# Attention in a fused layer: four single PSUM banks for the products of the row maximum, three for the scores, and one exponential per head

## The reference

```
hn = layernorm(x, ln1_g, ln1_b)
q, k, v = (hn @ wq + bq), (hn @ wk + bk), (hn @ wv + bv)     # split in 16 heads of 16
scores = einsum('bhqd,bhkd->bhqk', q, k) / sqrt(16)
attn = softmax(scores, axis=-1)
o = einsum('bhqk,bhkd->bhqd', attn, v)
...
x = x + o @ wo + bo         # then layernorm, argmax over 8 experts, the chosen expert's FFN
```

## Time and profile before

| | before |
|---|---|
| median of 3 runs | 3639.58 us (3636.05 to 3642.61) |
| the profiled execution, own time | 3635.68 us |
| its span | 3634.0 us |
| granted TensorE clock, mean | 0.894 |
| first and last value product of attention | 1498.6 and 2924.1 us |
| PE, DVE, ACT busy over the span | 83%, 72%, 48% |

### The profile page before, as it was taken

One profiled execution on the slowest core, in us unless ns is written; L12 is line 12 of the kernel. 1 busy time (PEld: TensorE's weight loads), 2 busy tenths in 40 slices (PEclk: granted clock), 3 DMA queues, 4 the chain that ended last, 5 costly groups with the idle time before them and its releaser, 6 DMA issues. The chain is left out here.

```text
span 3634.0 us, 43270 instructions
## 1 busy us (share of the span) xinstructions
PE 3014.5 (83%) x12860; PEld 1434.6 (39%) x12860; DVE 2601.1 (72%) x3622; ACT 1729.3 (48%) x2113; POOL 816.1 (22%) x397
## 2 busy tenths in 40 slices
PE   5668788787797775999999999999999957669994
PEld 3333234343343332433333333333333324658883
DVE  5526989789889896998989898989899638111111
ACT  2225554554544541376767676767677720101110
POOL 2204455455455465000000000000000015210003
PEclk9888899898898887799999999999999965589997
DMA  4532112111121124744545454445454044044554
GB/s 151 164 115 88 65 65 81 63 66 66 57 75 68 54 75 53 132 67 63 68 57 69 59 69 61 66 62 67 59 66 54 7 123 117 21 157 156 170 173 127
DMA packets 230405, 306.67 MB, mean 84 GB/s; under 512 B 111467, under 2 KB 179332, under 8 KB 215748
## 3 DMA queue, kind: packets, MB, share of 16 engines
q1 hardware_dynamic: 225988, 291.60, 35.3%
q0 software_dynamic: 4224, 12.59, 1.2%
HBM read 240.38 MB, written 63.21 MB: 84 GB/s over the span
## 5 line engine op out<-in xcount | busy, mean ns | idle before, releaser
L701 DVE TENSOR_REDUCE attn_mx<-attn_pX 128x1 f32<-128x512 f32 x2048 | 1271.0, 683 | 156.7 <-PE attn_pX L609 154.8
L681 ACT ACTIVATE attn_pr<-attn_pS 128x1024 f32<-128x1024 f32 x1024 | 992.8, 1022 | 500.0 <-PE attn_pS L622 499.4
L609 PE MATMUL attn_pX<-attn_ks,attn_qs 48*128 48x512 f32 x2048 | 749.8, 491 | 75.4 <-DMA attn_vs<-v_d 25.2
L1150 PE MATMUL mamba_pY<-mamba_g,mamba_ident 128*128 128x512 f32 x1024 | 523.4, 660 | 213.9 <-DVE mamba_g L1274 213.8
L1261 DVE TENSOR_TENSOR_SCAN mamba_h<-mamba_pA,mamba_hs,mamba_db 128x512 f32<-128x512 f32 x512 | 617.2, 1264 | 95.3 <-ACT mamba_pA L1004 90.3
L609 PEld LDWEIGHTS attn_pX<-attn_ks,attn_qs 48*128 48x128 f32 x2048 | 304.4, 190 | 773.2 <-DVE attn_mx L701 708.9
L945 POOL TENSOR_TENSOR mamba_db<-mamba_bq,mamba_u 128x2048 f32<-128x2048 f32 x128 | 577.8, 4515 | 72.5 <-DVE mamba_u L1221 72.2
L1004 ACT ACTIVATE mamba_pA<-mamba_dt,mamba_an 128x512 f32<-128x512 f32 x512 | 352.0, 691 | 456.2 <-DVE mamba_h L1261 455.9
L632 PE MATMUL attn_pO<-attn_pr,attn_vs 128*17 128x512 f32 x4096 | 549.5, 609 | 0.4 <-ACT attn_pr L681 0.4
L622 PE MATMUL attn_pS<-attn_qs,attn_ks 50*128 50x512 f32 x2048 | 467.7, 413 | 34.0 <-issue 19.8
L1150 PEld LDWEIGHTS mamba_pY<-mamba_g,mamba_ident 128*128 128x128 f32 x1024 | 209.4, 211 | 513.9 <-DVE mamba_g L1274 274.7
(11 more groups left out here) (170 smaller groups left out, 2027.5 us busy)
## 6 DMA issues: line engine op xcount, KB each, us to landing
mamba_bq<-bc_d SPq DMA_DIRECT2D x64, 1024.0 KB, 4.7
attn_ks<-parts_d SPq DMA_DIRECT2D x192, 256.0 KB, 9.3
exp_w<-in_w SPq DMA_DIRECT2D x46, 1024.0 KB, 4.9
attn_vs<-v_d SPq DMA_DIRECT2D x32, 544.0 KB, 15.5
parts_d<-proj_qp SPq DMA_DIRECT2D x32, 512.0 KB, 3.0
attn_qs<-parts_d SPq DMA_DIRECT2D x192, 64.0 KB, 8.3
attn_qs<-attn_mt SPq DMA_DIRECT2D x512, 1.0 KB
oraw_d<-attn_oe SPq DMA_DIRECT2D x32, 256.0 KB, 2.1
```

The costliest lines, as they stand in the source:

```text
L609: pe.matmul(pX[bank(s, n)][:, :], QS[slot][rows, pair, qt * P:(qt + 1) * P], KS[slot][rows, pair, part * BANK:(part + 1) * BANK], start=Tr ...
L681: act.activation(PR[2 * (kt % 2) + pair][:, :, :], pS[pair][:, :, :], ACT.Exp, scale=HD ** -0.5).then_inc(p_sb, 1)
L701: dve.tensor_reduce(MX[:, col:col + 1], pX[bank(s, n)][:, :], AX.X, ALU.max).then_inc(x_max, 1)
L1150: mm = pe.matmul(pY[j][:, :], ident[:, :], G[k % 2][:, n, :], start=False, stop=(q == NQ - 1 and n == QN - 1))
```

## The change

`pX` has 4 banks in place of 3. `pS` is 3 single banks in place of 2 double ones. Each head has its own exponential of 512 columns, and its own wait. The score products of a step go to the 3 banks in turn, so a score product waits for the exponential three places before it (`score_freed`). The counter of finished exponentials becomes two, for even and odd places. TensorE's order within a step changes: one head's score product, one X product, in turn; and the score product of the fourth head now stands behind the value products.

```diff
--- before.py
+++ after.py
@@ -449,9 +449,11 @@
     NG = batches * HEADS // GH
     NI = NG * QC
     RING = 4
-    NX = 3
+    NX = 4
+    NS = 3
     NSM = GH * QT * QC
     SM_KT = NSM // KT
+    NSC = GH * KT
     PAIRS = GH // 2
     MROWS = 2
     STACK_M = STACK + MROWS
@@ -472,7 +474,7 @@
         MS = m.sb("ms", [P, MROWS, GH * QT], F32R)
         MT = [m.sb(f"mt{n}", [P, 32]) for n in range(2)]
         ZERO = m.sb("zero", [P, slots_d.shape[1]])
-        pS = [m.ps(f"pS{n}", [P, 2, BANK]) for n in range(2)]
+        pS = [m.ps(f"pS{n}", [P, BANK]) for n in range(NS)]
         pX = [m.ps(f"pX{n}", [P, BANK]) for n in range(NX)]
         pO = m.ps("pO", [P, BANK])
         ops_in = [m.sem(f"ops_in{s}") for s in range(RING)]
@@ -486,7 +488,7 @@
         m_split = m.sem("m_split")
         m_turned = m.sem("m_turned")
         s_ps = m.sem("s_ps")
-        p_sb = m.sem("p_sb")
+        p_sb = [m.sem(f"p_sb{n}") for n in range(2)]
         pv_done = m.sem("pv_done")
         o_sb = m.sem("o_sb")
         o_out = [m.sem(f"o_out{n}") for n in range(2)]
@@ -501,6 +503,16 @@
                 return n - NX + 1
             before = [k - NSM for k in range(NSM) if bank(s - 1, k) == bank(s, n)]
             return max(before) + 1
+
+        def score_bank(s, n):
+
+            return (s % RING + n) % NS
+
+        def score_freed(s, n):
+
+            if n >= NS:
+                return n - NS
+            return max(k - NSC for k in range(NSC) if score_bank(s - 1, k) == score_bank(s, n))
 
         def order(n):
 
@@ -610,22 +622,23 @@
                                   KS[slot][rows, pair, part * BANK:(part + 1) * BANK],
                                   start=True, stop=True).then_inc(x_ps, 1)
 
-                def scores(i, s, kt, pair):
+                def scores(i, s, kt, h):
 
                     _, _, slot, use = where(i, s)
-                    if kt == 0 and pair == 0:
+                    if kt == 0 and h == 0:
                         pe.wait_ge(mrow_in[slot], use * MROW_IN + 2 * MROW_IN)
-                    z = s * 2 * KT + kt * 2 + pair
-                    pe.wait_ge(p_sb, i * (RING * 2 * KT) + (z + 1))
-                    for h in range(2):
-                        rows = slice(h * HALF, h * HALF + STACK_M)
-                        mm = pe.matmul(pS[pair][:, h, :], KS[slot][rows, pair, kt * P:(kt + 1) * P],
-                                       QS[slot][rows, pair, :], start=True, stop=True)
-                    mm.then_inc(s_ps, 1)
+                    n = kt * GH + h
+                    pair, half = divmod(h, 2)
+                    rows = slice(half * HALF, half * HALF + STACK_M)
+                    last = score_freed(s, n)
+                    pe.wait_ge(p_sb[last % 2], i * (RING * NSC // 2) + (s * NSC // 2 + last // 2 + 3))
+                    pe.matmul(pS[score_bank(s, n)][:, :], KS[slot][rows, pair, kt * P:(kt + 1) * P],
+                              QS[slot][rows, pair, :], start=True, stop=True).then_inc(s_ps, 1)
 
                 def values(i, s, kt):
 
-                    pe.wait_ge(p_sb, i * (RING * 2 * KT) + (s * 2 * KT + kt * 2 + 4))
+                    for n in range(2):
+                        pe.wait_ge(p_sb[n], i * (RING * NSC // 2) + (s * NSC // 2 + kt * 2 + 4))
                     if kt == 0:
                         pe.wait_ge(o_sb, i * RING + (s + 2))
                     for h in range(GH):
@@ -638,8 +651,8 @@
                 scores_max(0, 0, 0, NSM)
                 scores_max(0, 1, 0, LEAD)
                 pe.wait_ge(ones_ready, 2 * RING)
-                scores(0, 0, 0, 0)
-                scores(0, 0, 0, 1)
+                for h in range(GH):
+                    scores(0, 0, 0, h)
 
                 def maxima_ahead(i, s, left, n0, n1):
 
@@ -649,16 +662,20 @@
                     elif left >= 2:
                         scores_max(i, s + 2, n0 + LEAD - NSM, n1 + LEAD - NSM)
 
+                assert SM_KT == GH
+
                 def body(i, s, left):
                     for kt in range(KT):
                         n = kt * SM_KT
                         ahead = [(i, s, kt + 1)] if kt + 1 < KT else [(i, s + 1, 0)] if left >= 1 else []
-                        for pair in range(2):
+                        for h in range(GH - 1):
                             if ahead:
-                                scores(*ahead[0], pair)
-                            maxima_ahead(i, s, left, n + pair * SM_KT // 4, n + (pair + 1) * SM_KT // 4)
+                                scores(*ahead[0], h)
+                            maxima_ahead(i, s, left, n + h, n + h + 1)
                         values(i, s, kt)
-                        maxima_ahead(i, s, left, n + SM_KT // 2, n + SM_KT)
+                        if ahead:
+                            scores(*ahead[0], GH - 1)
+                        maxima_ahead(i, s, left, n + GH - 1, n + GH)
                 bodies(pe, body)
 
             @block.scalar
@@ -670,16 +687,18 @@
                     act.wait_ge(pv_done, i * (RING * KT) + (s * KT + 2))
                     act.copy(OE[n][:, :], pO[:, :]).then_inc(o_sb, 1)
 
-                act.sem_inc(p_sb, 2)
+                for n in range(2):
+                    act.sem_inc(p_sb[n], 2)
                 act.wait_ge(o_sb, 1)
 
                 def body(i, s, left):
                     for kt in range(KT):
                         act.wait_ge(pv_done, i * (RING * KT) + (s * KT + kt + 1))
-                        for pair in range(2):
-                            act.wait_ge(s_ps, i * (RING * 2 * KT) + (s * 2 * KT + kt * 2 + pair + 1))
-                            act.activation(PR[2 * (kt % 2) + pair][:, :, :], pS[pair][:, :, :], ACT.Exp,
-                                           scale=HD ** -0.5).then_inc(p_sb, 1)
+                        for h in range(GH):
+                            n = kt * GH + h
+                            act.wait_ge(s_ps, i * (RING * NSC) + (s * NSC + n + 1))
+                            act.activation(PR[2 * (kt % 2) + h // 2][:, h % 2, :], pS[score_bank(s, n)][:, :],
+                                           ACT.Exp, scale=HD ** -0.5).then_inc(p_sb[n % 2], 1)
                         if kt == 0:
                             copy_out(i, s)
                 bodies(act, body)
```

## The result

The changed kernel takes 3749.58 us, the median of 4 runs (3743.35 to 3793.66), against 3637.82 for the kernel before: 1.0335 times, 95% interval 1.0267 to 1.0404. Slower, as forecast, but by 112 us where I had 60 to 63; 3749.58 lies at the very end of the range that I gave. The profiled execution took 3743.35 us, its span is 3741.7, 107.7 more than before.

The account below looks back on a forecast made before the run. The loop of X products and VectorE reductions bound the kernel (2.69 us per step), to be replaced by a score loop of 2.83. Terms sum to +62.8 us: 3635.7 + 62.8 = 3698.5, predicted as 3700, range 3645 to 3750.

Parts of the forecast that it names:

- The X loop and its opening: X products and VectorE's reductions through three banks set the old step, 2.68 us by terms; a fourth bank opens this loop.
- The score loop, 2.83: Score product, X product, value products, fourth head's score product and last exponential form a closed loop of 2.83 us per step.
- The 468 steps: Attention steps left after taking off the last items', edge and half-clock steps; each grows from 2.69 to 2.83, +65.5 us.
- Halving costs nothing by itself: On ScalarE, the four extra exponential starts per step are hidden in idle time; 0.16 us per step were ScalarE the bound.
- Splits, -20: Steps with a split of maxima, one per item: VectorE's slack and the extra bank absorb the 0.70 us stall, -20 us.
- The last item, +8.9: Last item's steps, without X products, grow from 2.00 to 2.59 us: 15 x 0.59; five steps before it come back.
- Half-clock steps, +5.4: 16 steps behind the phase's start and loop edges lengthen from 4.13 to 4.47 us, +5.4 us.
- rival 4: One more 0.1 us delay per step, from value products' waits or more frequent half clock: +47 us, 3747; chance 0.11.
- Edges, +3: Restart at seven loop edges: an X product between last score product and values costs 0.43 us each, +3 us.
- 1: Rival: banks decouple the engines, so the step falls to VectorE's 2.40 us, about 3510 us in all; chance 0.07.
- rival 2: X product runs beside the score product, free in the score loop: step 2.59 us, 3586 us in all; chance 0.04.
- 3: Rival: the score loop closes at its short end, 2.74 us, 3656 to 3660, or 2.70 and 3640; chance 0.12.

Follow-up runs that it names:

- e4: Changed kernel with a zero bias from SBUF on each exponential, making it longer; fastest run 3783.7 us, the others 3858 to 4064, no ratio given.
- f1: Changed kernel with the X product before the value products moved ahead of the third head's score product; 3631.98 us, ratio 0.9980 to the kernel before.
- e1: Changed kernel with 3 X banks instead of 4; median 3898 us, fastest 3796.5 us, for that run alone ratio 1.0719 to the kernel before.
- e3: Kernel before with each 1024-column exponential split into two of 512, banks and order kept; 3639.75 us, ratio 1.0009.
- e2: Changed kernel with the fourth head's score product ahead of the value products instead of behind them; 3655.98 us, ratio 1.0050 to the kernel before.
- f2: Changed kernel with two of each step's four X products computed twice into the same bank; 3717.5 us, ratio 1.0213 to the kernel before.
- f3: Changed kernel with the hardware loop over the attention's rings written out, so without edges; 3694.5 us, ratio 1.0165 to the kernel before.
- g1: f1 with the ring loop written out and both sets of banks numbered on through all items; 3601.2 us, ratio 0.9885 to the kernel before.
- g3: Changed kernel's own order, ring loop written out, banks numbered on, unread filling products in the last item; 3673.1 us, ratio 1.0101 to the kernel before.
- g2: g1 plus filling X products in the last item, into idle banks that nobody reads; 3580.6 us, ratio 0.9845 to the kernel before.
- f4: Kernel before with the hardware loop over the attention's rings written out; 3602.8 us, ratio 0.9906.

## Why the prediction was right or wrong

**The X loop and its opening.** Right. With the loop of 2.68 open, VectorE does idle more and not less, since the score loop took over.

**The score loop, 2.83.** Right in length and in its terms. The step measures 2.83; ScalarE's gap is 0.77, where I had "about 0.6", and VectorE's 0.34, where I had "about 0.4": small misses in rows that follow from the step. e4 moved the step by the exponential's growth, f1 by the X product's 0.24, e1 showed the other loop next behind it. The term with no row of before, the exponential at 0.60, measured 0.604. The last item's 2.59 and the half-clock step's 4.47 came out too. The 468 steps made +66 us, as summed.

**Halving costs nothing by itself.** Right where ScalarE has slack, shown by e3.

**Splits, -20.** Right: -19.3. A step with a split is 0.09 over the others.

**The last item, +8.9.** Right for the profiled execution, with the five steps ahead of it +8.3 in all. That was partly luck: in the profiles of e2, f1, f2, f3 and g1 it ran at half clock, and the last 22 steps took 80 to 84 us there against 58 in the changed kernel's profile. Whether the slower of the changed kernel's four runs (3754.84 and 3793.66 us, granted clocks 0.877 and 0.865) had that or longer low stretches isn't known, as only one was profiled.

**Half-clock steps, +5.4.** This is the step that failed. I wrote "16 at half clock (two behind the phase's start and each edge)" and put the change into their length alone, 0.34 each. The length was right; the number was wrong, and I took it to be the same on both sides. The kernel before had 11, the changed one 35, and the term is +40. f2 gave the engine more to do in the same steps and their number fell to 10; f3 took away the edges, and outside the phase's start and the last item they vanished. What decides how long one stretch gets stays open: e1, with half-clock steps of 4.56, had five short ones and one of 92.2 us. I had the thought in rival 4, "a half clock that comes more often as TensorE idles more", and priced it as 0.1 us on every step. It is not on every step: it is 1.6 us on each step for which the clock stays down. That rival 4's 3747 lies so near the measured 3749.6 is luck, for its 0.1 on each of 468 steps did not come.

**Edges, +3.** Too small: +9.6. I counted seven stalls where there are six, and one slot of an X product at each. The first score product's wait at a ring's end, 7 x 0.48 = 3.4, and the fourth head's wait behind ScalarE's own stall, seen at 1885.37, came on top: the six stalls with it are 6.2 us longer in all.

Together the half-clock steps (35 us more than forecast) and the edges (6.6 more) are all but 3 us of what the forecast of +62.8 lacks on the +107.7 measured in the span. The table counts the 0.14 of all 511 steps in its first row, the forecast counted it in the terms of those steps; in the forecast's own terms the two misses are 37 and 7.6 us.

**The rivals.** 1, 2 and 3 did not come, as the step is 2.83; the 2.59 of rival 2 is real, but only with the X product elsewhere. A loop through the value products was left even with the fourth head ahead of them (e2), so three score banks did not give VectorE's 2.40 in any of the three orders run.

## What to carry to other kernels

Where engines hand banks round, the step is the longest closed path through a wait, and a product that stands in program order between two waits of that path is paid in full: one X product that took 0.24 us of each step made 92 us here (g3 against g2). Adding a bank opens one loop; before counting the gain, close the next one, from the place of each product in the engine's order. And count the steps at half clock as a result of the change, not as a property of the place: here the clock stayed down long after the stall at which it fell, in some executions and not in others, and more work on the same path went with shorter stretches.

## What the runs showed of the hardware that I had not expected

- The low clock's stretch behind the same stall differs from kernel to kernel and from edge to edge. It was 3.4 to 10.2 us in the kernel before (half-clock steps up to 4.13 us), and up to 13.7 us in e2 and f1 (up to 4.07). With 4.47 us it was 10.2 to 34.1 us (changed), with 4.55 and 4.56 us mostly 3.4 to 10.2 but once 300 us (e4) and once 92 us (e1). With two X products more per step at an unchanged step it was 3.4 to 10.2 us (f2). Behind edges, stretches over 13.7 us came only with half-clock steps of 4.47 us or more and no added products; these are six edges or fewer of one profile each.
- The times spread with the granted clock: 3634 to 3645 us over 13 runs of the kernel before at 0.891 to 0.895; 3743 to 3794 at 0.880 to 0.865 for the changed one; 3784 to 4064 at 0.884 to 0.793 for e4. The changed kernel's order without edges spread over 3691 to 3698 alone (f3).
- In the last item, with score and value products alone, the clock fell and stayed at half with steps of 4.04 to 4.10 us in five profiles (e2, f1, f2, f3, g1); in the profile of the changed kernel the same item ran at 2.59. Products that nobody reads, in idle banks, took 20.6 us off the whole.
- Far shorter idle times than those at an edge can stand ahead of a fall of the clock: three of 1.12 to 1.23 us, for a DMA (g1 once, g2 twice). Behind the same wait in the other items, with 0.92 us at most, it stayed at full clock.
- Writing out the loop over seven rings cost nothing that shows, and saved 34 us (f4).
